# Expert weights in pieces of 256 KB, earlier loads over the shared weights, and own rows for padding, in a one-core mixture-of-experts kernel

## The reference

```
x  = x + linear0(x * ys) * d                      # ys, d from the condition, by batch
shared = silu(x @ w1) * (x @ w3) @ w2             # 512 -> 1024 -> 512
s  = sigmoid(concat(x, t) @ router_W);  topk 2 of (s + bias);  gates = s_sel / sum
y_e = gelu(x @ W1e[e], exact) @ W2e[e]            # 512 -> 512 -> 512
x  = x + (shared + sum of gate * y_e over the two) / 3
```

## Time and profile before

| | us |
|---|---|
| median of 3 timed runs | 1079.09 (1078.06 to 1082.4) |
| the profiled execution's own time | 1082.94 |
| its span, first to last instruction | 1081.1 |
| TensorE busy, share of the span | 1030.0, 95% |
| VectorE, ScalarE, GpSimd busy | 507.4, 292.7, 332.3 |
| mean granted TensorE clock | 0.983 |

### The profile page before, as it was taken

How to read it: one execution, slowest core, us unless ns; L and a number is a source line. 1 busy time by engine, 2 the same in 40 slices (tenths; PEclk the granted TensorE clock), 3 DMA queues, 4 the chain that set the end, 5 groups by cost and what they waited for, 6 DMA issues and landing times.

```text
span 1081.1 us, 14559 instructions
## 1 busy us (share of the span) xinstructions
PE 1030.0 (95%) x4692; PEld 841.7 (78%) x4692; DVE 507.4 (47%) x829; ACT 292.7 (27%) x461; POOL 332.3 (31%) x385
## 2 busy tenths in 40 slices
PE   6999999999999999999999995989999999999993
PEld 5888778887888888888888883878888887878782
DVE  4565456577324324324232123555555555555452
ACT  3222252332222222222111122223333333233230
POOL 1000000001113424334324102445545555555532
PEclk9999999999999999999999998999999999999997
DMA  5566587768867676877735629997779999999963
GB/s 177 195 216 228 205 285 258 243 242 237 280 217 263 209 271 225 244 276 238 235 96 155 134 78 282 294 266 136 155 135 197 238 200 230 219 223 213 210 126 56
DMA packets 132026, 226.77 MB, mean 210 GB/s; under 512 B 28848, under 2 KB 83760, under 8 KB 122864
## 3 DMA queue, kind: packets, MB, share of 16 engines
q1 hardware_dynamic: 59168, 142.22, 40.9%
q0 software_dynamic: 31328, 64.11, 26.2%
q10 hardware_dynamic: 41472, 19.68, 8.2%
HBM read 111.01 MB, written 96.54 MB: 192 GB/s over the span
## 4 chain that ended last, share of the span: by engine, by line
PE 75%; DMA 16%; DVE 3%; issue 3%; ACT 1%; SPq 1%; POOLq 0%; POOL 0%; DVEq 0%
DMA we<-we_d 12%; PE banks L466 10%; PE banks L467 10%; PE banks L468 10%; PE banks L528 7%; PE banks L530 7%; PE banks L529 7%; PE banks L480 5%; PE banks L481 5%; PE banks L482 5%; DMA out<-ys,slot 4%; PE banks L414 3%; PE banks L415 3%; PE banks L416 3%; PE banks L446 1%
## 5 line engine op out<-in xcount | busy, mean ns | idle before, releaser
L466 PE MATMUL banks<-xh,w13h 128*128 128x512 f32 x512 | 200.1, 391 | 1.8 <-DVE xl L723 1.8
L468 PE MATMUL banks<-xh,w13l 128*128 128x512 f32 x512 | 199.9, 390 | 0.0
L467 PE MATMUL banks<-xl,w13h 128*128 128x512 f32 x512 | 199.9, 390 | 0.0
L1184 POOL DMA_INDIRECT out<-ys,slot x71 | 123.9, 1745 | 202.5 <-DMA out<-ys,slot 118.8
L791 DVE SCALAR_TENSOR_TENSOR gm<-sil,banks 128x512 f32<-128x512 f32 x64 | 43.9, 687 | 248.2 <-ACT sil L609 248.2
L528 PE MATMUL banks<-we,hidth 128*128 x284 | 114.3, 402 | 16.2 <-issue 15.2
L1071 DVE TENSOR_TENSOR hidtl<-hidt,hidth 128x512 fp32r<-128x512 f32 x71 | 49.2, 693 | 161.6 <-ACT hidth L683 161.6
L609 ACT ACTIVATE sil<-banks 128x512 f32<-128x512 f32 x64 | 38.3, 598 | 314.8 <-PE banks L468 314.8
L1170 POOL DMA_DIRECT2D xg<-xs_d x136 | 99.9, 1113 | 63.1 <-DMA out<-outst 51.0
L528 PE MATMUL banks<-we,xgth 128*128 x284 | 111.4, 392 | 5.0 <-issue 4.4
L466 PEld LDWEIGHTS banks<-xh,w13h 128*128 128x128 f32 x512 | 96.7, 189 | 22.4 <-issue 2.3
(11 more groups left out here) (163 smaller groups left out, 1465.0 us busy)
## 6 DMA issues: line engine op xcount, KB each, us to landing
we_d<-ehl SPq DMA_DIRECT2D x32, 1024.0 KB, 6.4
hturn<-hid ACTq DMA_DIRECT2D x284, 64.0 KB
xg<-xs_d POOLq DMA_DIRECT2D x136, 128.0 KB
eraw<-expert_w SPq DMA_DIRECT2D x32, 512.0 KB, 5.0
we<-we_d SPq DMA_DIRECT2D x8, 2048.0 KB, 10.3
we<-we_d SPq DMA_DIRECT2D x32, 512.0 KB, 6.2
x1t_d<-x1t SPq DMA_DIRECT2D x8, 1024.0 KB, 8.6
xin<-x1t_d SPq DMA_DIRECT2D x8, 1024.0 KB, 9.4
```

What stands on the lines that cost most here:

```text
L466: pe.matmul(ps[hc % 2][:, :], w_hi, xh[:, j, c, :], start=(c == 0), stop=False)
L467: pe.matmul(ps[hc % 2][:, :], w_hi, xl[:, j, c, :], start=False, stop=False)
L468: last = pe.matmul(ps[hc % 2][:, :], w_lo, xh[:, j, c, :], start=False, stop=(c == DC - 1))
L1184: pool.indirect_dma_start(out[:, :], IO(slot[:, t, 0:1], 0), ys[:, t % RING, :], None, compute_op=ALU.add).then_inc(added[t % 2], 16)
```

## The change

1. **Late weights in 256 KB parts.** `load_in_parts` now makes eight DMAs of 256 KB per half instead of four of 512 KB, still waiting for each before the next (L337 of the changed kernel). It is used for halves 4 to 7 too, which were one DMA of 2 MB each. For turns 4 to 7 there are 64 loads instead of 32.
2. **Shared weights give way by chunk.** High and low part of a chunk's `w1`/`w3` now lie side by side in one tensor `w13`, so that two chunks make the room of one expert half. Halves 1, 2 and 3 (2 MB each) are asked for in block 7, when `ab_done` is 58, 60 and 62. Half 4 is asked for at 64, in parts, and `store_out(7)` stands behind its eighth part.
3. **x asked for sooner.** GpSimd's `load_pair(2)` and `load_pair(3)` stand ahead of the waits on `waits_done`, `out_stored` and the new wait on `pads_in`.
4. **Own rows for padding.** The output has 1024 spare rows instead of 128 (`PADS` is 8). GpSimd writes another row number into the padding record before each of its 8 scatters. The zero rows for them (2 MB instead of 256 KB, DRAM to DRAM) are stored in block 1 instead of at the start. The table `wait_for` no longer has the condition `tail`: of two neighbouring tiles of the last turn the later one need not wait for the earlier, padding tiles included.

```diff
-PADROWS = P
 PADS = (SLOTS - K * TOK) // P
+PADROWS = PADS * P
...
-        w13h = sb("w13h", [HC, 2, DC, P], FP32R, 16)
-        w13l = sb("w13l", [HC, 2, DC, P], FP32R, 48)
+        w13 = sb("w13", [HC, 2, 2 * DC * P], FP32R, 16)
...
-            sp.dma_start(out[TOK:TOK + PADROWS, :], padrows).then_inc(pads_in, 16)
...
+                    if n == 1 and hc == 3:
+                        sp.dma_start(out[TOK:TOK + PADROWS, :], padrows).then_inc(pads_in, 16)
...
             def load_in_parts(i, e, place):
 
-                for q in range(4):
-                    sp.dma_start(we[:, bass.ds(place, 1), i % 2, q // 2, q % 2]...
-                    sp.wait_ge(we_in[i % HRING], 16 + 16 * (q + 1))
+                for q in range(8):
+                    half, part, c = q // 4, q // 2 % 2, q % 2
+                    sp.dma_start(we[:, place, i % 2, half, part, c]...
+                    sp.wait_ge(we_in[i], parts_before[i] + 16 * (q + 1))
+                parts_before[i] += 128
                 sp.sem_inc(weights_in, 1)
...
-            sp.wait_ge(ab_done, HC * NBLK)
-            load_weight(1, first[0], slice(0, 1))
-            store_out(NBLK - 1)
-            weight_loaded(1)
-
-
-            for i in range(2, HRING):
+            for i in (1, 2, 3):
+                sp.wait_ge(ab_done, HC * (NBLK - 1) + 2 * i)
                 load_weight(i, first[i // 2], slice(i // 2, i // 2 + 1))
                 weight_loaded(i)
+            sp.wait_ge(ab_done, HC * NBLK)
+            load_in_parts(4, first[2], slice(2, 3))
+            store_out(NBLK - 1)
+            for i in range(5, HRING):
+                load_in_parts(i, first[i // 2], slice(i // 2, i // 2 + 1))
             for r in range(WRING, E):
...
                 for i in (2 * r, 2 * r + 1):
-                    load_in_parts(i, e, place)
-            sp.wait_ge(pads_in, 16)
+                    load_in_parts(i % HRING, e, bass.ds(place, 1))
...
-                then(dve.tensor_scalar(tail[0:1, :], at, used, None, ALU.is_lt))
-                then(dve.tensor_tensor(same[0:1, 1:TILES], same[0:1, 1:TILES], tail[0:1, 1:TILES], ALU.mult))
...
             for g in range(PADS):
                 if g:
                     pool.wait_ge(pad_out, 16 * g)
+                pool.tensor_copy(xrow[:, XB - 1, D:D + 1].bitcast(INT32), padtok[:, g:g + 1]).then_inc(pad_put, 1)
+                pool.wait_ge(pad_put, g + 1)
                 pool.indirect_dma_start(xs_d[:, :], IO(padr[:, g:g + 1], 0), xrow[:, XB - 1, :], None).then_inc(pad_out, 16)
...
-            pool.wait_ge(waits_done, 1)
...
-            pool.wait_ge(out_stored, 16 * NBLK)
             load_pair(2)
             load_pair(3)
+            pool.wait_ge(waits_done, 1)
+            pool.wait_ge(pads_in, 16)
+            pool.wait_ge(out_stored, 16 * NBLK)
             for t in range(TILES):
```

More of the change, by code:

```diff
@@ L111, in shared_moe_kernel @@
         same = sb("same", [TILES], INT32, 196.5)
-        tail = sb("tail", [TILES], INT32, 197)
         x1tok = sb("x1tok", [BLK // Q, DC, Q], FP32, 168)
@@ L153, in shared_moe_kernel @@
         padr = small("padr", [PADS], INT32)
+        padtok = small("padtok", [PADS], INT32)
         pad = small("pad", [3, 2 * E])
@@ L216, in shared_moe_kernel @@
         xrow_out = [sem(f"xrow_out{b}") for b in range(XB)]
-        rec_put, pad_done, zero_in, pad_out = sem("rec_put"), sem("pad_done"), sem("zero_in"), sem("pad_out")
+        rec_put, pad_put, pad_done, zero_in, pad_out = sem("rec_put"), sem("pad_put"), sem("pad_done"), sem("zero_in"), sem("pad_out")
         xg_in = [sem(f"xg_in{j}") for j in range(2)]
@@ L329, in load_weight @@
                              we_d[bass.ds(e * 4 + i % 2 * 2, 2)].rearrange("h p s n -> p h (s n)").bitcast(FP32)).then_inc(we_in[i % HRING], 16)
+            parts_before = [16 if i < 4 else 0 for i in range(HRING)]
             def load_in_parts(i, e, place):
-                for q in range(4):
-                    sp.dma_start(we[:, bass.ds(place, 1), i % 2, q // 2, q % 2].rearrange("p a c n -> p (a c n)").bitcast(FP32),
-                                 we_d[bass.ds(e * 4 + i % 2 * 2 + q // 2, 1), :, q % 2].rearrange("a p n -> p (a n)").bitcast(FP32)).then_inc(we_in[i % HRING], 16)
-                    sp.wait_ge(we_in[i % HRING], 16 + 16 * (q + 1))
+                for q in range(8):
+                    half, part, c = q // 4, q // 2 % 2, q % 2
+                    sp.dma_start(we[:, place, i % 2, half, part, c].rearrange("p a n -> p (a n)").bitcast(FP32),
+                                 we_d[bass.ds(e * 4 + i % 2 * 2 + half, 1), :, part, c * D:(c + 1) * D].rearrange("a p n -> p (a n)").bitcast(FP32)).then_inc(we_in[i], 16)
+                    sp.wait_ge(we_in[i], parts_before[i] + 16 * (q + 1))
+                parts_before[i] += 128
                 sp.sem_inc(weights_in, 1)
@@ L464, in up @@
                     for c in range(DC):
-                        w_hi, w_lo = w13h[:, hc, m, c, :], w13l[:, hc, m, c, :]
+                        w_hi, w_lo = (w13[:, hc, k, (m * DC + c) * P:(m * DC + c + 1) * P] for k in range(2))
                         pe.matmul(ps[hc % 2][:, :], w_hi, xh[:, j, c, :], start=(c == 0), stop=False)
@@ L594, in _ @@
                 act.wait_ge(wraw_in[n % 2], 16 * (n // 2) + 16)
-                act.activation(w13h[:, n].rearrange("p m c n -> p (m c n)"), wraw[:, n % 2, :], ACT.Copy).then_inc(w_high, 1)
+                act.activation(w13[:, n, 0, :], wraw[:, n % 2, :], ACT.Copy).then_inc(w_high, 1)
             def w2_high(g):
@@ L767, in _ @@
                 dve.wait_ge(w_high, n + 1)
-                w_hi = w13h[:, n].rearrange("p m c n -> p (m c n)").bitcast(FP32)
-                dve.tensor_tensor(w13l[:, n].rearrange("p m c n -> p (m c n)"), wraw[:, j, :], w_hi, ALU.subtract).then_inc(w_split, 1)
+                dve.tensor_tensor(w13[:, n, 1, :], wraw[:, j, :], w13[:, n, 0, :].bitcast(FP32), ALU.subtract).then_inc(w_split, 1)
             def w2_low(g):
@@ L924, in pad_rows @@
                 then(dve.tensor_tensor(dst[:, 0:PADS], dst[:, 0:PADS], place, ALU.add))
+                then(dve.tensor_scalar(padtok[:, :], tid[:, 0:PADS], float(TOK), None, ALU.add))
                 dve.tensor_copy(padr[:, :], dst[:, 0:PADS]).then_inc(pad_done, 1)
@@ L1080, in scatter_waits @@
             def scatter_waits():
-                at, used = cst[0:1, C_TIX:C_TIX + TILES], e8[0:1, 1, E - 1:E]
-                then(dve.tensor_scalar(wait_for[0:1, :], at, 1.0, None, ALU.add))
+                then(dve.tensor_scalar(wait_for[0:1, :], cst[0:1, C_TIX:C_TIX + TILES], 1.0, None, ALU.add))
                 then(dve.tensor_scalar(wait_for[0:1, :], wait_for[0:1, :], 1, 255, ALU.logical_shift_right, ALU.bitwise_and))
                 then(dve.tensor_tensor(same[0:1, 1:TILES], turn_of[0:1, 1:TILES], turn_of[0:1, 0:TILES - 1], ALU.is_equal))
-                then(dve.tensor_scalar(tail[0:1, :], at, used, None, ALU.is_lt))
-                then(dve.tensor_tensor(same[0:1, 1:TILES], same[0:1, 1:TILES], tail[0:1, 1:TILES], ALU.mult))
                 then(dve.tensor_tensor(same[0:1, 1:TILES], wait_for[0:1, 1:TILES], same[0:1, 1:TILES], ALU.subtract))
@@ L1142, in _ @@
             pool.wait_ge(pad_done, 1)
-            pool.dma_start(xrow[:, XB - 1, 0:D], padrows).then_inc(zero_in, 16)
+            pool.dma_start(xrow[:, XB - 1, 0:D], padrows[0:P]).then_inc(zero_in, 16)
             pool.dma_start(xrow[:, XB - 1, D:ROW].bitcast(INT32), padslots[:, 0:2]).then_inc(zero_in, 16)
```

## The result

The changed kernel takes 1109.11 us in the median of 4 runs (1103.47 to 1110.67), the kernel before 1080.17 in 4 runs beside it. The ratio is 1.0258, with a 95% interval of 1.0215 to 1.0301. The forecast was 1089 us, slower, in a range of 1061 to 1112, with 1080 to 1102 as its likeliest case: the measured time lies outside the likeliest case and 3 us inside the range.

The account below looks back on a forecast made before the run. TensorE, busy 95% of the span, bounds the kernel before. Wins of 8.8 and 3.2 us put its last matmul at 1053 and scatters at 1061, but SP's loads end at 1090: median 1089 us, range 1061 to 1112.

Parts of the forecast that it names:

- likeliest case: SP's late weight loads at 4.6 to 5.2 us each, giving medians of 1080 to 1102 us; chance 0.50.
- SP's chain as the new end: SP's 64 one-by-one loads of turns 4 to 7 end the kernel at 1090 us, 29 us after the last scatter.
- The price of a load beside the tiles: Turns 4 to 7: each 256 KB load takes 4.9 us while tiles run, between bounds of 2.9 and 6.0.
- third rival: Late weight loads: every part pays in full, a constant addition; 5.4 us a load, median 1107 us; chance 0.14.
- Halves 4 to 7 in by the time of turn 4: Their 32 parts from 641.4 us, up to 5 us each, are in when turn 4 starts at 803 us.
- Start of the routed stage: `matmul2(0)` starts at 664.7 us instead of 670.80; with clock and restart TensorE wins 8.8 us.
- the signs: Marks expected in the profile, among them a gap before `matmul2(0)` under 1 us and a clock there about 1.0.
- Gaps of the tiles: TensorE's 10 us of idle gaps from 676 to 1066 us: a third given back, 3.2 us, bounds -4 and 8.
- Scatters of the padding: End of kernel: with two in flight, scatters end at 1060 to 1061 us; 8 of 15.8 us go.
- x sooner: Start of routed stage: GpSimd issues x of pair 2 at 645 us, 10 us sooner, and it is no longer last.
- Zeros, copies, table, layout at nothing: 2 MB of zeros in block 1, eight GpSimd copies, two VectorE table steps and the `w13` layout cost 0 us.
- the first, a hidden chain: SP's loads stay hidden and the scatters end the kernel; at 3.9 us a load, median 1060 us; chance 0.22.

Follow-up runs that it names:

- run 1: The changed kernel with turns 4 to 7 in 512 KB parts again (32 loads instead of 64), halves 4 to 7 still in 256 KB parts; 1058.91 us, ratio 0.9812.
- run 2: The kernel before with only turns 4 to 7 in 64 loads of 256 KB; 1115.49 us, ratio 1.0313.
- run 3: The changed kernel without the 64 loads of turns 4 to 7, which no tile reads with the inputs as drawn; 1056.71 us, ratio 0.9799.
- run 4: The changed kernel with two of the 256 KB parts of turns 4 to 7 in flight instead of one; 1058.47 us, ratio 0.9811.
- run 8: The kernel before with only halves 1 to 3 early; halves 4 to 7 as 2 MB each, store behind the issue of half 4; 1074.49 us, ratio 0.996.
- run 5: The kernel before with only own output rows for the padding, including the zeros in block 1; 1070.89 us, ratio 0.9924.
- run 6: The kernel before with only x of pairs 2 and 3 asked for ahead of the waits; 1077.23 us, ratio 0.9984.
- run 7: The kernel of run 1 without x sooner and without own rows for padding; 1085.01 us, ratio 1.0063 to the kernel before.
- run 11: The changed kernel with turns 4 to 7 in 128 loads of 128 KB; 1233.32 us.
- run 12: The changed kernel with turns 4 to 7 in 16 loads of 1 MB; 1063.19 us.

## Why the prediction was right, step by step

- **SP's chain as the new end**: shown from both sides, by runs 1 to 4. It was the one term that gave the forecast its sign, and it came from a list in which the unchanged kernel had 52 us to spare. That the time would be longer was a judgement all the same: the sign turned at 4.7 us a load, the bounds were 2.9 and 6.0, and the forecast gave "slower" 0.61.
- **The price of a load beside the tiles**: mis-sized. Taken was 4.9 us between bounds of 2.9 and 6.0; measured 5.5. The 5.5 lies outside the forecast's own 4.6 to 5.2 and belongs to its third rival, to which it gave 0.14. "I take 4.9 us, nearer to 4.3" is the step that failed: it let the waiting shrink with the load. Near the tiles' end 3.9 was taken and 4.2 measured, alone 2.9 and 3.3 (the fastest landing of the earlier trace rows was no typical one). At the measured prices 16 loads remain when TensorE is through instead of 12.3, and take 3.3 us each: 52 us instead of 36. That is the 16 us by which the span of 1106.7 exceeds the 1091 of the sum. In medians the difference is 20 us, 1109 to 1089: the other 4 are the 3.9 us by which the profiled execution before stood above its median. The forecast took them off again, but the changed kernel's profiled execution stands 0.6 below its median.
- **Halves 4 to 7 in by the time of turn 4**: not quite, and the right start of turn 4 is luck. They take 640 to 804 us with the table reading behind them, 5.1 us each with the store between. The 25th tile's `matmul2` starts its last matmul at 799.97, and turn 4 starts at 804.28 with no wait for TensorE: the halves set it, not the tiles, as the third rival had it. The forecast's 803 came from the tiles. In run 1 the same halves hold turn 4 until 808.80, and there it costs nothing.
- **Start of the routed stage**: `matmul2(0)` was put at 664.7 and starts at 663.90. The steps came as told: x of pair 2 is asked for at 644.06 (645 in the forecast), the hidden part of tile 0 is transposed at 658.62 without a wait (658), and ScalarE's DMA issues hold its high part until 662.30 (663.2). But two of the signs failed: the gap before `matmul2(0)` is 2.04 us and not under 1, and the granted clock from 655 to 669 us is 0.76 and not about 1.0. The second part of that term, 2.4 us for 12 matmuls back at full clock, did not come. In the chain of the changed kernel TensorE works at 0.43 us a matmul already from 655 us:

```profile
654.47 0.50 PE banks L531
655.20 0.35 PE banks L533
655.55 0.43 PE banks L531
655.98 0.43 PE banks L532
...
661.85 2.04 issue
663.90 0.49 PE banks L531
```

Matmuls 0.43 us apart are those at 1.2 GHz; some eight come from 655 us on and some eight again from 665 us, behind the wait of 2.04. The gaps ahead of the first, 0.6, 0.3 and 1.9 us, are no longer than those of the kernel before at that place (0.6 and 2.2 in the earlier trace rows, then 1.7), and there the clock held until the long wait. Why it fell sooner is open.

- **Gaps of the tiles**: 3.2 us were given back, and from the start of `matmul2(0)` to TensorE's last matmul it is 386.9 us instead of 394.5: 7.5, near the bound of 8 and mis-sized. The forecast gave a share of all gaps to "fewer bytes at once"; run 8 shows 4.5 of them in one place, 676 to 727 us, and that the early halves remove them, not the small parts. The errors at the start and in the gaps partly cancel: TensorE's last start was put at 1053 and came at 1050.8.
- **Scatters of the padding**: put at 1060 to 1061 for the last landing; run 1, which they end, has a span of 1058.1 with TensorE 2.3 us ahead of the forecast. Run 5 shows 8.6 us by medians for this part alone, where the forecast had 8.
- **x sooner**: x is no longer late, as forecast. What the forecast didn't price: alone it turns one wait into another (run 6), and without it the moved store costs more than the rest wins (run 7).
- **Zeros, copies, table, layout at nothing**: run 5 has the first three and gains in full. In the changed kernel the last `up` ends no later than before: SP's first load behind `ab_done` 64 goes out at 639.98, before at 641.38. The layout had no run of its own; run 8 has it and wins.
- **Rivals**: the first, a hidden chain, would have given 1060: run 4 is what it would look like (1058.47), but it takes two in flight. The third, every part in full, was the nearest, at 5.4 us a load and 1107. Its reason, one addition for all sizes, doesn't hold, see below.

## What to carry to other kernels

A queue that loads one piece at a time has a rate of its own, piece over latency, and beside other traffic the latency fell much less than the size here: halving the piece took 1.2 us off 6.7. Before cutting pieces, count them, take the price with neighbours running, and set the sum against the slack at that queue's last wait; where small pieces are wanted, keep two in flight. Loads that nobody reads are on the path too, if the program waits for them.

## What the runs showed of the hardware

The time from issue to issue of one load, waited for each time, 128 partitions, from runs 1, 2, 11, 12 and the changed kernel:

| part | beside the tiles | alone | addition |
|---|---|---|---|
| 128 KB | 4.2 us | 2.7 | 1.5 |
| 256 KB | 5.5 | 3.1 to 3.3 | 2.3 |
| 512 KB | 6.7 | 3.4 (3.2 of the earlier trace rows and 0.2) | 3.3 |
| 1 MB | 8.5 | no run | |

Beside the tiles a doubling adds 1.3, 1.2 and 1.8 us. The column has SP's table readings in it, one in 47 distances at 128 KB but three in 15 at 1 MB. At the 1.75 us each of the forecast's estimate (7 us for four) it would be 4.1, 5.4, 6.5 and 8.2. The 512 KB "alone" is the fastest load of another tensor and not a mean, so its addition is, if anything, too large. The addition is neither constant, as the third rival had it, nor in proportion to the bytes: it grows by somewhat under 1 us with each doubling. The Trainium skill, "DMA: Bandwidth & Descriptors", section "Queues, rings and completion order", has the engines go round the queues by whole packets; all these loads have 128 rows of 1 to 8 KB. Read as the third rival read it, with every part paying the same turns at the round, the addition should stay. The measurement decides: in the mean it falls with the bytes in a row too, and of the 256 KB parts a good third pay next to nothing while a third pay some 4 us.

Not expected was how little the tiles mind. Between 812 and 1010 us the DMA engines' share is 0.74 without weight loads, 0.99 with 512 KB parts and 1.00 with two of 256 KB in flight (by the fast execution of run 4), and TensorE makes 859, 853 and 866 matmuls. The fewest, 848, are those of run 12 with 1 MB parts. The traffic delayed the queue with one load in flight and hardly the tiles. That the four-deep buffers of the tiles are the reason is likely and was not tested.
